# Which of two waits a TensorE job carries, and three ScalarE constants as immediates, in a four-engine pipeline on one core

## The reference

```python
h = tok(x)                       # three state-space layers; after layers 0 and 1 the steps are averaged in pairs
h = h + attn(layernorm(h))       # linear attention by a Taylor series, 8 heads of 8
h = h + ffn(layernorm(h))        # router and 6 experts, the best 2 of them summed
# one state-space layer:
dbc = einsum('ble,ce->blc', x, W_dbc); delta, Bm, Cm = split(dbc)
delta = softplus(delta * W_dt + b_dt)
h_t = exp(delta * A) * h_(t-1) + (delta * x) * Bm ;  y = sum_n(h_t * Cm) + D * x
# the attention, for normalized q and k (qn, kn) of each head, with s = qn . kn:
y = sum over keys of (0.5 * s**2 + scale**2 * s + scale**4) * [1, v] / N ;  out = y[1:] / y[0]
```

## Time and profile before

| What | Value |
|---|---|
| time, median of 3 runs | 648.1 us (646.14, 648.12, 648.1) |
| span of the profiled execution | 644.8 us |
| PE busy | 572.2 us (89%), 9531 matmul records |
| DVE busy | 540.6 us (84%) |
| ACT busy | 525.0 us (81%) |
| POOL busy | 423.5 us (66%) |
| chain that ended last, by engine | PE 44%, ACT 19%, DVE 17%, POOL 9%, issue 5% |

### The profile page before, as it was taken

The page is one execution under the profiler, slowest core; times in us unless marked ns, Lnnn a source line. Parts: engine busy times, 40 slices in busy tenths (PEclk is TensorE's granted clock), DMA queues, the critical chain, the costliest instruction groups (busy, mean ns, idle before and its releaser), DMA issues.

```text
span 644.8 us, 22886 instructions
## 1 busy us (share of the span) xinstructions
PE 572.2 (89%) x9531; PEld 302.5 (47%) x9531; DVE 540.6 (84%) x1019; ACT 525.0 (81%) x1044; POOL 423.5 (66%) x549
## 2 busy tenths in 40 slices
PE   3777778999999999999999999999999999999972
PEld 2333234545455555455445455455545545545431
DVE  5898999999899899989898999999898987764441
ACT  1345668989899999998898998999999888888761
POOL 7758899788867677768567766767686755423110
PEclk9998879999999999999999999999999999999998
DMA  3432222221220213230211212220221001000001
GB/s 78 83 82 63 65 59 59 61 52 31 52 48 20 56 43 77 47 74 14 69 31 45 55 44 61 58 47 15 68 49 29 5 8 31 17 14 14 2 14 29
DMA packets 77575, 28.52 MB, mean 44 GB/s; under 512 B 69271, under 2 KB 77463, under 8 KB 77463
## 3 DMA queue, kind: packets, MB, share of 16 engines
q1 hardware_dynamic: 71290, 25.92, 17.6%
q10 hardware_dynamic: 6173, 1.05, 0.9%
HBM read 13.25 MB, written 3.05 MB: 25 GB/s over the span
## 4 chain that ended last, share of the span: by engine, by line
PE 44%; ACT 19%; DVE 17%; POOL 9%; issue 5%; DMA 2%; ACTq 2%; SPq 1%; POOLq 0%; DVEq 0%
PE ring L1274 7%; PE ring L1353 5%; ACT pm L1057 5%; PE ring L1366 4%; PE ring L1461 4%; DVE ring L1714 3%; PE ring L1260 3%; PE ring L1432 2%; PE ring L1441 2%; ACT hid L1100 2%; PE ring L1229 2%; PE ring L1249 2%; PE ring L1336 1%; PE ring L1412 1%; DVE carry_C L1710 1%
## 5 line engine op out<-in xcount | busy, mean ns | idle before, releaser
L1057 ACT ACTIVATE pm<-ring,two_col 93x744 f32<-93x744 f32 x128 | 107.4, 873 | 10.0 <-PE ring L1353 9.0
L1353 PE MATMUL ring<-q_exp,qk 32*93 32x372 f32 x512 | 56.4, 507 | 7.7 <-ACT ln_rows_a L1021 1.1
L1821 DVE TENSOR_TENSOR hidw<-hid,ring 128x744 f32<-128x744 f32 x48 | 44.3, 922 | 19.1 <-PE ring L1422 11.5
L911 POOL TENSOR_TENSOR q_exp<-qk,mask_q 128x1488 f32<-128x1488 f32 x16 | 42.9, 2683 | 22.2 <-DVE qk L1772 22.2
L1366 PE MATMUL ring<-pm,v 97*32 97x93 f32 x2048 | 53.7, 245 | 1.2 <-ACT pm L1057 0.4
L1100 ACT ACTIVATE hid<-ring,b_col 128x372 f32<-128x372 f32 x96 | 49.3, 568 | 1.5 <-PE ring L1441 0.9
L1366 PEld LDWEIGHTS ring<-pm,v 97*32 97x32 f32 x2048 | 42.4, 109 | 15.3 <-ACT pm L1057 3.4
L1107 ACT ACTIVATE hid<-ring,b_col 128x744 f32<-128x744 f32 x48 | 42.2, 879 | 8.9 <-PE ring L1432 6.4
L1432 PE MATMUL ring<-hid,w 64*64 64x372 f32 x384 | 40.3, 489 | 3.2 <-ACT hid L1100 2.7
L896 POOL TENSOR_TENSOR base_C<-base_C,carry_C 128x744 f32<-128x744 f32 x16 | 28.5, 1781 | 20.1 <-DVE carry_C L1723 9.5
L1441 PE MATMUL ring<-nrm_f,w 64*64 64x372 f32 x384 | 40.0, 486 | 0.2
(11 more groups left out here) (368 smaller groups left out, 1755.4 us busy)
## 6 DMA issues: line engine op xcount, KB each, us to landing
xin_A<-in_x_dram SPq DMA_DIRECT2D x62, 93.0 KB
xin_B<-in_x_dram SPq DMA_DIRECT2D x62, 93.0 KB
x_A<-x_A SPq DMA_DIRECT2D x32, 93.0 KB, 2.4
x_B<-x_B SPq DMA_DIRECT2D x32, 93.0 KB, 2.2
x_C<-x_C SPq DMA_DIRECT2D x32, 93.0 KB, 2.2
out_dram<-osb SPq DMA_DIRECT2D x15, 186.0 KB
x_D<-x_D SPq DMA_DIRECT2D x32, 46.5 KB, 2.2
w<-in_L_ffn_expert_w_dram SPq DMA_DIRECT2D x6, 48.0 KB
```

The source lines that it names most:

```text
L1057: a.activation(pm[q % 2][h][0:TOUT].rearrange("m a j n -> m a (j n)"), out_of(f"att.s{q}{h}", g)[0:TOUT, :, 0:COLS], ACT.Square, bias=two_ ...
L1353: ins = mm(o[h][0:TOUT, b, 0:COLS], qk[r:r + 32, 1, q * TOUT:(q + 1) * TOUT], q_exp[r:r + 32, q].rearrange("p j n -> p (j n)"), start=True ...
L1821: tt(hidw[k][:], hid2[:], out_of(f"ffn.g_{k}", g)[:, :, 0:COLS], ALU.mult).then_inc(me, 1)
```

## The change

No engine's list of jobs changes: the five lists hold the same jobs in the same order, and the banks are the same. Their text is laid out anew. In PE's list 768 of 1000 entries get a mark `!`. For a marked job `bank` is called ahead of the job's own code, so the bank's waits are written ahead of the data's. Where both kinds are left after `need` has dropped what is already known, this exchanges them: the bank's wait now sits on the first weight load, and the data's wait stands alone ahead of it. A job with two banks can have a wait for each of two engines (the scores of L1353 often do); `bank` goes through a Python set, so which of these two is written first is not fixed by the code and can differ from one build to the next. Where data and bank are on the same engine, the bank's count can cover the data's, and the separate wait falls away. Most marked jobs have one wait or none, and there nothing changes.

The three columns go: lnv, rnorm and pm on ACT take their bias as a number, and DVE fills three columns fewer.

```diff
-        two_col = sb("two_col", [P, 1])
-        ln_col = sb("ln_col", [P, 1])
-        eps_col = sb("eps_col", [P, 1])
...
-                    "att.s0:0/0,4 A.s:3/6 C.c:2/2 B.dpre:4/4 A.xT:4/0 C.s:2/4 att.cen:1/6 att.y0:0/2 att.s2:0/0,6 A.b:3/2 "
...
+                    "att.v:0/7! att.s0:0/0,4 A.s:3/6! C.c:2/2! B.dpre:4/4! A.xT:4/0! C.s:2/4! att.cen:1/6! att.y0:0/2! "
...
+        FIRST = {tuple(entry.split("/")[0].split(":")) for entry in ORDER["pe"].split() if entry[-1] == "!"}
...
-            BANK |= {(job, int(g_)): int(b) for job, b in zip(PAIRED.get(w_, (w_,)), banks_.split(","))}
+            BANK |= {(job, int(g_)): int(b) for job, b in zip(PAIRED.get(w_, (w_,)), banks_.rstrip("!").split(","))}
...
-                    a.activation(ln_rows[w][:], out_of(f"{u}.var", g)[:, 0, 0:TOUT], ACT.Ln, bias=eps_col[:]).then_inc(me, 1)
+                    a.activation(ln_rows[w][:], out_of(f"{u}.var", g)[:, 0, 0:TOUT], ACT.Ln, bias=LN_EPS).then_inc(me, 1)
...
-                    a.activation(qk_norm[:], qk_norm[:], ACT.Exp, bias=ln_col[:], scale=-0.5).then_inc(me, 1)
+                    a.activation(qk_norm[:], qk_norm[:], ACT.Exp, bias=12.0 * LN2, scale=-0.5).then_inc(me, 1)
...
                     a.activation(pm[q % 2][h][0:TOUT].rearrange("m a j n -> m a (j n)"),
                                  out_of(f"att.s{q}{h}", g)[0:TOUT, :, 0:COLS], ACT.Square,
-                                 bias=two_col[0:TOUT], scale=0.5 ** 0.5).then_inc(me, 1)
+                                 bias=2.0, scale=0.5 ** 0.5).then_inc(me, 1)
...
             def do(g, u, s):
+                if (f"{u}.{s}", str(g)) in FIRST:
+                    for job in PAIRED.get(f"{u}.{s}", (f"{u}.{s}",)):
+                        bank(g, job)
                 {"att": attention, "ffn": experts, "prep": prepare}.get(u, ssm)(g, u, s)
...
-            for t_, val in ((zero_col, 0.0), (clamp_col, CLAMP), (under_col, -UNDERFLOW),
-                            (two_col, 2.0), (ln_col, 12.0 * LN2), (eps_col, LN_EPS)):
+            for t_, val in ((zero_col, 0.0), (clamp_col, CLAMP), (under_col, -UNDERFLOW)):
...
-            consts = 13 + 6 + 14 + NX + len(cleared) + 4
+            consts = 13 + 6 + 11 + NX + len(cleared) + 4
```

## The result

The changed kernel takes 650.46 us (median of 20 runs, 647.37 to 652.69), the kernel before 646.94 us (median of 20 runs, 645.2 to 649.42). The ratio is 1.0048, with a 95% interval from 1.0034 to 1.0063: the change makes the kernel slower by some 3 us, where 4.2 us less than 648.1 were forecast. The profiled execution of the changed kernel has a span of 648.7 us, against 644.8.

The account below looks back on a forecast made before the run. No single engine bounds it: PE, DVE and ACT are nearly full and the chain keeps changing engine. Constants 5.2, waits 1.3 and scores 0.5 make 7.0 us; 60%, 4.2, gives 643.9 against 648.1; range 641.1 to 647.1.

Parts of the forecast that it names:

- the three constants: Part on lnv, rnorm and pm on ACT: number operands save 5.2 us of the chain; DVE's fewer memsets save nothing.
- the third: Rival: slower by the clock, a low-clock stretch moving into the full middle; 652.9 us if it lasts 20 us; chance 0.05.
- The general sentence: On what bounds the kernel: with every list's order kept, shortening one operation starts none later, apart from contention and the clock.
- The constants' price: On ACT: a column operand costs 90 ns; pm would fall from 873 to 780 to 790 ns, lnv from 341 to near 250.
- the 15.8: ACT's whole busy time: 176 instructions at 0.09 us each, 15.8 us less of 525.0.
- The sum on the chain: Constants 5.2, exchanged waits 1.3 and scores 0.5 make 7.0 us on the old chain; 60% of it, 4.2 us, was taken.
- 60% of 5.2: Constants on the chain: 58 ACT operations at 0.09 us make 5.2 us, of which the estimated share of 60% was taken.
- 60% of 1.8: Waits at hand-overs to PE: 1.8 us on the chain, of which 60%, 1.1 us, was taken.
- The exchanged waits: Hand-overs to PE: 0.09 us gained at 16, lost at two z jobs behind data that comes last; net 1.3 us.
- half was taken: Scores with two bank waits: half of 11 chain hand-overs lose their 0.09 us, 0.5 us, ends 0 and 1.0.
- The clock: Granted clock 1.00 throughout the full middle, 100 to 600 us; below 1.00 there would show the prediction wrong.
- The absorbed case: First rival: ACT just idles more, only exchanged waits and stretches where ACT is last pay; 646.9 us; chance 0.15.

Follow-up runs that it names:

- g1: Changed kernel with three unused columns just ahead of the input tiles, so only constants and weights stay 96 bytes lower; 644.31 us, ratio 0.9939.
- g2: Changed kernel with three unused columns behind the input tiles, so weights and input tiles stay 96 bytes lower; 650.36 us, ratio 1.0044.
- e2: Kernel before with its three columns allocated behind all other tiles, so the tiles in between stand 96 bytes lower; 654.87 us, ratio 1.0107.
- e1: Changed kernel with three unused columns where the removed ones stood, so every later tile keeps its old address; 643.88 us, ratio 0.9940.
- e4: Kernel before with only the three constants as numbers, columns still allocated but unused, old waits; 643.95 us, ratio 0.9944.
- e3: Kernel before with only the new order of the waits, columns still in use at their old places; 647.90 us, ratio 0.9993.
- j1: Changed kernel, old places up to sel, five unused columns ahead of the input tiles and one behind (xin_A at 38944, remainder 32 by 256); 650.54 us, ratio 1.0056.

## Why the prediction was wrong

**The step that failed** is in the part on the three constants: "DVE fills three columns fewer at the start. [...] nothing". Of the three columns only the memsets were counted, not the bytes. With them every later tile moved, the input tiles from a remainder of 128 to one of 32, and that costs 6.0 us (g1 to g2), 6.8 us in the kernel of before (e2). The forecast was 4.2 us faster; 648.1 - 4.2 + 6.0 = 649.9, and with the 6.8 of e2 it is 650.7; measured is 1.0048 x 648.1 = 651.2. The DMA that the sentence leaned on, which the first matmul waits for, itself ends some 1 us later in the five kernels with such a remainder. No rival held it: the third, the only slower one, was the clock, and e1 at the same clock takes 643.9 us. The general sentence, that the time "can start others earlier and none later, apart from contention and the clock", leaned on durations that stay what they are. The DMA's didn't.

**The constants' price was right.** 90 ns for each operand: `pm` 783 ns, `lnv` 251 ns. Summed instruction by instruction, ACT's durations fell by 16.0 us (607.65 to 591.69), as the 15.8 said: 11.5 for the 128 `pm` (107.4 - 95.9), 2.9 for the 32 `lnv`, 1.5 for the 16 `rnorm` (449 to 358 ns). ACT's busy time, which counts overlapping instructions once, fell by 12.1: the other 3.9 us were overlap (82.7 us of it before, 78.8 now).

**The sum on the chain came out, its parts can't be told.** e1 has the 4.2 us (648.11 to 643.88) that were forecast for the two parts together. But the constants alone bring 4.2 (e4), where 60% of 5.2, 3.1, was taken, and the waits 0.2 (e3), where 60% of 1.8, 1.1, was. By the medians the 60% was too low for the one and too high for the other, but neither is shown: e4's interval, 2.3 to 4.9 us, holds the 3.1 and e3's holds the 1.1. That the total hit 4.2 is in part luck.

**The exchanged waits do what was read.** At the exchanged places the 0.14 is gone from the chain, and it appears at `z` behind the swaps' DMAs. Why so little of it reaches the time is not shown.

**L1353: half was taken, less came.** 11 of 20 hand-overs had the 0.14, 7 of 19 have it now, but pieces between 0.04 and 0.14 took the place of some: all issue pieces ahead of it sum to 2.0 us before and 1.9 now, where 0.5 less was taken.

**The clock** stayed at 1.00 from 100 to 600 us, as was said, and lay between 0.76 and 0.95 in the first 100 us, with no relation to the times (e1 has 0.81, j1 0.76, the kernel before 0.91).

**The absorbed case** (646.9 us) is refuted by e4: ACT's shorter operations shorten the kernel by about a third of the 12.1 us, and the upper end of e4's interval, 0.9964, is 645.8 us.

## What to carry to other kernels

A buffer that is taken out or put in moves all that is allocated behind it; compare the addresses of the tiles that DMAs write, and test an edit with the freed bytes held by a dummy before its effect is read. When a change that touches no transfer makes the same packets and bytes take more of the DMA engines' time, look at the addresses first. And where packets are 256 bytes, keep their destination in SBUF off the places 32 bytes behind or ahead of a multiple of 256: one unused column of 32 bytes (i2) turned the changed kernel from 0.5% slower into 0.45% faster. This rule comes from one kernel and one pattern of loads.

## What was not expected of the hardware

- A write of 256-byte packets into SBUF at an address 32 or 224 behind a multiple of 256: 19.8 to 20.1 ns for a packet in place of 17.9 to 18.3, in five kernels against ten, and 6 us of 650 in a kernel whose DMA engines are busy only 18% of the time.
- Packets that lie across the multiple of 256 with 64 + 192, 96 + 160 or 128 + 128 bytes on its sides: 18.0 ns between 100 and 200 us, as whole ones (18.0).
- Stores of 256-byte packets out of SBUF: 17.65 to 17.77 ns where the tile read starts on a multiple of 256, 18.96 to 19.63 at five other remainders, with nothing seen of it in the kernel's time.
- The wait that comes last, alone in an instruction ahead of a weight load: the job ends some 90 ns later than with the wait on the weight load (in the chain of before, issue piece and job: L1353 0.14 + 0.88 against 0.04 + 0.88 us, L1274 0.14 + 0.86 against 0.04 + 0.85). It is real at each hand-over and yet the exchanged waits together changed the kernel's time by less than could be measured.
